# Three of a row's eight routed weight pairs through seven half-row block products, and layer 1 with its channels on the partitions

## The reference, cut to what matters

```python
def _gemma_mlp(x, gate_w, up_w, down_w):
    g = jnp.einsum('bsh,hi->bsi', x, gate_w)
    u = jnp.einsum('bsh,hi->bsi', x, up_w)
    return jnp.einsum('bsi,ih->bsh', jax.nn.gelu(g, approximate=True) * u, down_w)
...
rw = jax.nn.softmax(router_logits, axis=-1)
w, sel = jax.lax.top_k(rw, 2)
w = w / w.sum(axis=-1, keepdims=True)
...
x = x + sum_e dense_w[:, e] * mlp_e(x) + mlp_shared(x)
out = jnp.einsum('btc,oc->bto', x, W_base) + b_base
h = jnp.einsum('btc,erc->bter', x, As)
lora = jnp.einsum('bter,eor,be->bto', h, Bs, w)
x = x + out + lora * 2.0
```

## Time and profile before

| | |
|---|---|
| median of three runs | 812.03 us (811.63 to 812.24) |
| the profiled execution | 812.84 us |
| its span, first to last instruction | 811.0 us |
| TensorE busy | 804.5 us (99%), granted clock 1.00 in every slice |
| VectorE busy | 557.0 us (69%) |
| ScalarE busy | 402.1 us (50%) |
| GpSimd busy | 85.9 us (11%) |
| DMA | 80.34 MB, mean 99 GB/s |

### The profile page before, as it was taken

How to read it: one execution, slowest core, us unless ns; L and a number is a source line. 1 busy time by engine, 2 the same in 40 slices (tenths; PEclk the granted TensorE clock), 3 DMA queues, 4 the chain that set the end, 5 groups by cost and what they waited for, 6 DMA issues and landing times.

```text
span 811.0 us, 11123 instructions
## 1 busy us (share of the span) xinstructions
PE 804.5 (99%) x3666; PEld 670.8 (83%) x3666; DVE 557.0 (69%) x808; ACT 402.1 (50%) x659; POOL 85.9 (11%) x66
## 2 busy tenths in 40 slices
PE   9999999999999999999999999999999999999998
PEld 7788888888887888888888888888888888888886
DVE  4886987987876575666766666665666656667554
ACT  5574564554653544445445445444454445454442
POOL 1441321321111000100100010010001001001000
PEclk9999999999999999999999999999999999999999
DMA  6330521303211723433343244244225333333200
GB/s 200 86 113 12 147 77 18 114 0 104 91 39 53 221 87 108 131 118 103 104 146 102 78 147 125 79 132 138 93 88 167 91 104 129 121 99 104 66 0 27
DMA packets 92293, 80.34 MB, mean 99 GB/s; under 512 B 32864, under 2 KB 85856, under 8 KB 92256
## 3 DMA queue, kind: packets, MB, share of 16 engines
q1 hardware_dynamic: 92256, 79.88, 31.9%
HBM read 67.28 MB, written 12.58 MB: 98 GB/s over the span
## 4 chain that ended last, share of the span: by engine, by line
PE 98%; DVE 1%; ACT 0%; issue 0%; POOL 0%; DVEq 0%; ACTq 0%; POOLq 0%
PE ps_ring L587 61%; PE ps_acc L587 34%; PE ps_ring L707 1%; PE ps_acc L767 0%; DVE wide L1122 0%; PE ps_acc L701 0%; DVE xc L1122 0%; DVE sh_dn L1122 0%; ACT wide L872 0%; PE ps_acc L787 0%; PE ps_ring L605 0%; DVE stage L1456 0%; ACT stage L967 0%; PE ps_ring L609 0%; PE ps_ring L613 0%
## 5 line engine op out<-in xcount | busy, mean ns | idle before, releaser
L587 PE MATMUL ps_ring<-xc,wide 128*128 128x512 f32 x2220 | 529.4, 389 | 0.3 <-DVE post L1164 0.3
L587 PEld LDWEIGHTS ps_ring<-xc,wide 128*128 128x128 f32 x2220 | 415.6, 188 | 86.3 <-issue 0.7
L872 ACT CAST inner_hi<-post 128x512 fp32r<-128x512 f32 x192 | 118.1, 622 | 295.6 <-DVE post L1385 229.5
L1122 DVE TENSOR_TENSOR inner_lo<-post,inner_hi 128x512 fp32r<-128x512 f32 x192 | 135.5, 713 | 88.5 <-ACT inner_hi L872 88.2
L587 PE MATMUL ps_acc<-inner_hi,wide 128*128 128x512 f32 x504 | 175.8, 389 | 0.9 <-ACT stage L967 0.9
L1385 DVE SCALAR_TENSOR_TENSOR post<-post,coef_now,ps_ring 128x512 f32<-128x512 f32 x128 | 95.3, 744 | 55.8 <-PE ps_ring L587 54.8
L587 PEld LDWEIGHTS ps_acc<-inner_hi,wide 128*128 128x128 f32 x504 | 94.6, 188 | 21.0 <-ACT stage L967 1.4
L587 PE MATMUL ps_acc<-inner_lo,wide 128*128 128x512 f32 x252 | 98.0, 389 | 0.0
L1071 ACT ACTIVATE post<-ps_ring 128x512 f32<-128x512 f32 x128 | 76.0, 594 | 39.9 <-PE ps_ring L587 39.8
L1122 DVE TENSOR_TENSOR wide<-xbuf,wide 128x1024 fp32r<-128x1024 f32 x64 | 68.8, 1115 | 24.8 <-ACT wide L872 24.8
L1122 DVE TENSOR_TENSOR wide<-raw,wide 128x1024 fp32r<-128x1024 f32 (+2 forms) x70 | 64.4, 957 | 30.9 <-ACT wide L872 30.9
(11 more groups left out here) (100 smaller groups left out, 415.2 us busy)
## 6 DMA issues: line engine op xcount, KB each, us to landing
raw<-n_L_cond_skill_gate_dram SPq DMA_DIRECT2D x32, 256.0 KB, 2.9
raw<-in_L_cond_skill_up_dram SPq DMA_DIRECT2D x32, 256.0 KB, 3.5
raw<-n_L_cond_skill_down_dram SPq DMA_DIRECT2D x32, 256.0 KB, 3.8
xbuf<-n_L_cond_skill_gate_dram SPq DMA_DIRECT2D x32, 256.0 KB, 2.9
xbuf<-in_L_cond_skill_up_dram SPq DMA_DIRECT2D x32, 256.0 KB, 3.4
xbuf<-n_L_cond_skill_down_dram SPq DMA_DIRECT2D x32, 256.0 KB, 3.7
xt_scratch<-xbuf SPq DMA_DIRECT2D x8, 512.0 KB, 3.3
sh_scratch<-stage SPq DMA_DIRECT2D x8, 512.0 KB, 2.7
```

The lines of the kernel that those rows point to most:

```text
L587: last = pe.matmul(dst, left_[a], right_[b], start=start and n == 0, stop=stop and n == len(PASSES) - 1, skip_group_check=adds)
L872: return nc.scalar.copy(dst, src)
L1122: return V.tensor_tensor(dst, src, hi.bitcast(F32), ALU.subtract)
```

## The change

Pairs 3, 5 and 7 of each row (`SEVEN`) no longer make 4 times 6 matmuls of 512 columns for gate and up. Instead the row's tokens are cut in two halves of 256 (`HS`), each weight in its four 128 by 128 blocks, and `seven_products` makes seven products, each of them for gate and for up side by side in one bank: 7 x 2 x 3 = 42 matmuls of 256 columns. Both chunks of the pair are done at once; then come the two `down` that are due. For this

- POOL makes the sums of the tokens once a row (`sums_of_x`, 4 operations of 256 columns) and of the weights for each of the three pairs (`sums_of_weights`, 4 operations of 256 columns), and one of the output blocks (`ex_c22`, 512 columns); ACT and DVE split the sums (1024 columns each time);
- ACT copies two banks out (`ex_copy_out`), DVE adds four times a bank (`ex_seven`), and gelu and multiply work on pieces of 256, 256 and 512 columns;
- the weights of a pair are split in one piece of 1536 columns, at the chunks of a table (`SPLIT_AT`), and the splits stand ahead of the chunk's own `inner_lo` instead of behind it; for pairs 3, 5 and 7 `weights_ready` comes with the split of the sums;
- `layer1` of rows 0 to 6 makes 12 matmuls of 512 columns with the channels on the partitions; ACT adds the bias (`add_bias`), DVE transposes within blocks of 32 (`turn_output`), and SP stores a row in 8 transfers of 64 KB with runs of 128 bytes (`store_blocks`);
- `fold` goes from chunk 12 to chunk 9, `w_eff` from chunks 13 and 14 to 12 and 13, and layer 1's constants are loaded earlier in row 0 and to other memory; they are still taken in at one chunk of row 0 (`CONST_STEP`), now chunk 4 instead of 7.

```diff
+    SEVEN = [3, 5, 7]
+    NS = len(SEVEN)
+    HS = S // 2
...
+        SPLIT_AT = {0: 2, 2: 3, 5: 4, 6: 5, 9: 6, 10: 7, 13: 8, 14: 9}
+        SUMS_AT = {2 * pr - 2: n_s for n_s, pr in enumerate(SEVEN)}
...
+            def sums_of_weights(b, n_s):
+                s_, j = divmod(SEVEN[n_s], PAIRS)
+                st = b * NS + n_s
+                pool.wait_ge(raw_landed[j], b * (48 * TOP_K) + 48 * (s_ + 1))
+                pool.wait_ge(weights_ready, b * (TOP_K * PAIRS) + (SEVEN[n_s - 1] + 1 if n_s else SEVEN[-1] + 1 - TOP_K * PAIRS))
+                v = raw_gu(j).rearrange("p (g c i) -> p g c i", g=2, c=HC)
+                a11, a12 = v[:, :, 0, P:PW], v[:, :, 1, P:PW]
+                a21, a22 = v[:, :, 0, 0:P], v[:, :, 1, 0:P]
+                s1, s2, s3, s4 = (s_tmp[:, :, n, :] for n in (S1, S2, S3, S4))
+                G.tensor_tensor(s1, a21, a22, ALU.add).then_inc(ex_s1_made, 1)
+                G.tensor_tensor(s3, a11, a21, ALU.subtract)
+                pool.wait_ge(ex_s1_made, 2 * st + 1)
+                G.tensor_tensor(s2, s1, a11, ALU.subtract).then_inc(ex_s1_made, 1)
+                pool.wait_ge(ex_s1_made, 2 * st + 2)
+                G.tensor_tensor(s4, a12, s2, ALU.subtract).then_inc(ex_s_made, 1)
...
+            def ex_c22(b, n_s):
+                st = b * NS + n_s
+                pool.wait_ge(ex_v_done, st + 1)
+                pool.wait_ge(ex_u1_done, st + 1)
+                G.tensor_tensor(ex_v, ex_v, ex_u1, ALU.add).then_inc(ex_c22_done, 1)
...
+            def row(b, first):
+                sums_of_x(b, first)
+                sums_of_weights(b, 0)
                 pool.wait_ge(base_landed, b * 16 + 16)
-                pool.wait_ge(xf_landed, b * 16 + 16)
                 G.tensor_tensor(base, base, xf, ALU.add).then_inc(base_ready, 1)
-            with pool.Fori(0, B) as i:
-                row(i)
+                for n_s in range(NS):
+                    ex_c22(b, n_s)
+                    if n_s < NS - 1:
+                        sums_of_weights(b, n_s + 1)
+            row(0, True)
+            with pool.Fori(1, B) as i:
+                row(i, False)
...
+            def seven_products(b, par, k, n_s):
+                st = b * NS + n_s
+                for n, (bank, a_, b_, opens) in enumerate(PRODUCTS):
+                    if n == 0:
+                        pe.wait_ge(gelu_done, whole(b, k - 1))
+                    elif n == 1:
+                        pe.wait_ge(ex_t_ready, b + 1)
+                        pe.wait_ge(mul_done, whole(b, k - 1))
+                    elif n == 2:
+                        pe.wait_ge(mul_done, whole(b, k))
+                    elif n == 3:
+                        pe.wait_ge(gelu_done, whole(b, k))
+                    elif n in (4, 5):
+                        pe.wait_ge(ex_copied, 2 * st + n - 3)
+                    else:
+                        pe.wait_ge(ex_v_done, st + 1)
+                    for part in (GATE, UP):
+                        last = product(ring[bank][:, part * HS:(part + 1) * HS],
+                                       [ex_left(n_s, hl, part, a_) for hl in range(2)],
+                                       [ex_right(par, hl, b_) for hl in range(2)],
+                                       opens and part == GATE, True, True)
+                    last.then_inc(ex_product, 1)
+            def down_chunk(k):
...
             def layer1(b):
                 pe.wait_ge(x1_ready, b + 1)
                 pe.wait_ge(w_eff_ready, b + 1)
-                for t in range(TT):
+                for m in range(HC):
                     for c in range(HC):
-                        last = product(ps_misc[t // 2][:, t % 2 * H:(t % 2 + 1) * H],
-                                       [v[:, c, t * P:(t + 1) * P] for v in x1_s],
-                                       [w[:, c * H:(c + 1) * H] for w in w_eff_s], c == 0, c == HC - 1)
-                    if t % 2 == 1:
-                        last.then_inc(l1_done, 1)
+                        last = product(ps_misc[m][:], [w[:, c * H + m * P:c * H + (m + 1) * P] for w in w_eff_s],
+                                       [v[:, c, :] for v in x1_s], c == 0, c == HC - 1)
+                    last.then_inc(l1_done, 1)
...
+                    if k // 2 in SEVEN:
+                        if k % 2 == 0:
+                            seven_products(b, par, k, SEVEN.index(k // 2))
+                            down(b, k - 2)
+                            down(b, k - 1)
+                        continue
...
             def split_routed(b, s, j, freed, count):
-                split_routed_gu(b, s, j, freed, count)
-                split_routed_dn(j)
+                act.wait_ge(raw_landed[j], b * (48 * TOP_K) + 48 * (s + 1))
+                act.wait_ge(freed, count)
+                take_hi(ex_all(0, j), raw[j]).then_inc(weights_hi, 1)
...
+            def ex_copy_out(b, n_s, first):
+                st = b * NS + n_s
+                if n_s == 0:
+                    if first:
+                        act.wait_ge(turned_w, 1)
+                        act.wait_ge(a_ready, 1)
+                    else:
+                        act.wait_ge(o_ready, b * 2)
+                for n, to, bank in ((0, ex_u1, 0), (1, ex_v, 2)):
+                    act.wait_ge(ex_product, st * NP + n + 1)
+                    if n == 0:
+                        act.wait_ge(ex_mul, 3 * st)
+                    nc.scalar.copy(to, ring[bank][:]).then_inc(ex_copied, 1)
...
+            def ex_gelu_of(b, k, n_s):
+                st = b * NS + n_s
+                act.wait_ge(ex_product, st * NP + 5)
+                act.wait_ge(mul_done, whole(b, k))
+                gelu_of(gelu[0][:, 0:HS], ring[0][:, 0:HS]).then_inc(ex_gelu, 1)
+                act.wait_ge(ex_c_done, 2 * st + 1)
+                gelu_of(gelu[0][:, HS:S], ex_c12[:, 0:HS]).then_inc(ex_gelu, 1)
+                act.wait_ge(ex_c_done, 2 * st + 2)
+                act.wait_ge(ex_c22_done, st + 1)
+                gelu_of(gelu[1].rearrange("p (t n) -> p t n", t=2), ex_c2[:, :, 0:HS]).then_inc(ex_gelu, 1)
...
+            def ex_seven(b, k, n_s):
+                st = b * NS + n_s
+                s = k // IC
+                dve.wait_ge(ex_product, st * NP + 3)
+                dve.wait_ge(ex_copied, 2 * st + 2)
+                V.tensor_tensor(ex_v, ring[3][:], ex_v, ALU.add).then_inc(ex_v_done, 1)
+                dve.wait_ge(ex_product, st * NP + 4)
+                V.tensor_tensor(ex_u1, ring[1][:], ex_u1, ALU.add).then_inc(ex_u1_done, 1)
+                dve.wait_ge(ex_gelu, 3 * st + 1)
+                dve.wait_ge(inner_ready, b * K + k)
+                ex_inner(b, s, inner[0][:, 0:HS], gelu[0][:, 0:HS], ring[0][:, HS:S])
+                dve.wait_ge(ex_product, st * NP + 6)
+                dve.wait_ge(ex_u1_done, st + 1)
+                V.tensor_tensor(ex_c12, ring[2][:], ex_u1, ALU.add).then_inc(ex_c_done, 1)
+                dve.wait_ge(ex_product, st * NP + 7)
+                dve.wait_ge(ex_c22_done, st + 1)
+                V.tensor_tensor(ex_u1, ring[3][:], ex_u1, ALU.add).then_inc(ex_c_done, 1)
+                dve.wait_ge(ex_gelu, 3 * st + 2)
+                dve.wait_ge(ex_c_done, 2 * st + 1)
+                ex_inner(b, s, inner[0][:, HS:S], gelu[0][:, HS:S], ex_c12[:, HS:S])
+                dve.wait_ge(ex_gelu, 3 * st + 3)
+                dve.wait_ge(ex_c_done, 2 * st + 2)
+                ex_inner(b, s, inner[1].rearrange("p (t n) -> p t n", t=2),
+                         gelu[1].rearrange("p (t n) -> p t n", t=2), ex_c2[:, :, HS:S])
                 for i in range(2):
-                    dve.wait_ge(l1_done, b * 2 + i + 1)
-                    V.tensor_tensor(o_row[:, 2 * i:2 * i + 2, :],
-                                    ps_misc[i][:].rearrange("p (t h) -> p t h", t=2),
-                                    bias[:].unsqueeze(1).to_broadcast([P, 2, H]), ALU.add)\
-                        .then_inc(o_ready, 1)
+                    dve.wait_ge(inner_hi, b * K + k + i + 1)
+                    take_lo(inner_s[1][:, k % 4 + i, :], inner[i], inner_s[0][:, k % 4 + i, :])                        .then_inc(inner_ready, 1)
             def row(b, par, first, last):
+                def split_pair(k):
...
-                take_lo(ex_gu_all(1, j), raw_gu(j), ex_gu_all(0, j))
-                take_lo(ex_dn_all(1, j), raw_dn(j), ex_dn_all(0, j)).then_inc(weights_ready, 1)
+                last = take_lo(ex_all(1, j), raw[j], ex_all(0, j))
+                if s * PAIRS + j not in SEVEN:
+                    last.then_inc(weights_ready, 1)
```

More of the change, by code:

```diff
@@ L480, in row @@
                         .then_inc(layer1_landed, 16)
+                    store_shared(Q - 1)
+                else:
+                    sp.wait_ge(x1_done, b * 2)
+                    sp.wait_ge(sh_stored, 16 * B)
+                    sp.dma_start(base, sh_dram[b]).then_inc(base_landed, 16)
+                load_routed(b, 1, range(2, PAIRS))
                 if not last:
@@ L830, in row @@
```

(20 more changed lines are left out.)

264 lines of the change are left out of this document (193 added, 71 removed).

## The result

The changed kernel takes **806.35 us** (median of 6 runs, 805.82 to 807.56) beside 812.13 for the kernel before (6 runs, 811.56 to 812.41). The ratio is 0.9932, 95% interval 0.9922 to 0.9942: 0.7% faster. The forecast was 807.8 (801.2 to 815.0), with a chance of 0.66 for faster. The profiled execution has a span of 804.7 us where the one before had 811.0.

What follows compares the result with a forecast made beforehand. TensorE, busy throughout the routed stage, was taken as the bound. Terms -9.5 - 1.1 + 4.9 + 1.5 = -4.2 took the profiled 812.84 to 808.6, stated as 807.8 us against the 812.03 median; range 801.2 to 815.0.

Steps and rivals of the forecast that it cites:

- seven products, 24 pairs: TensorE's gate and up: a pair falls from 5.44 to 5.04 us, 24 times over 8 rows: -9.5 us.
- `layer1`, 7 rows: TensorE in rows 0 to 6: 2.88 us becomes 2.72, 0.16 x 7 = -1.1 us.
- wait for `layer1_sum`: TensorE idle 0.7 us before the next row's first down, seven times: +4.9 us.
- row 0: Layer 1's constants and both first splits of sums in chunk 4 delay pair 3's product 2: +1.5 us.
- the walk: Pair 7's first product to the next row's first down: TensorE wants x1_done at 18.64 us, VectorE finishes at 19.3.
- turns: VectorE operations with both inputs in SBUF wait for GpSimd's whole operation: 0.55 us each, six before layer1_sum.
- All of it arrives: Rival: two turns fewer, or VectorE 0.7 us earlier at the walk's start; full -10.6 gives 801.4 us; chance 0.18.
- Given back: Rival: one turn more, TensorE waiting 1.07 to 1.5 us a row; 810.4 to 813.7 us; chance 0.17.
- Slower: VectorE becomes the bound: Rival: multiplies reading a bank also take turns with GpSimd, up to 1.0 us more per row: 814.8 us; chance 0.17.
- It doesn't do what it says: Rival: 256-column matmuls take over 129 ns between waits; chance counted within the given-back and slower cases.

Runs made afterwards that it cites:

- experiment 4: Kernel before with the change's layer 1 alone (512-column matmuls, bias on ScalarE, transposes, eight stores): 811.0 us, ratio 0.9984.
- experiment 1: The change with GpSimd's four sums of the next row's tokens made to wait until behind layer1_sum: 802.14 us, ratio 0.9874.
- Experiment 5: Kernel before with, in row 0 alone, pair 2's split ahead of chunk 0's high and low parts: 810.76 us, ratio 0.9988.
- experiments 2 and 10: 2: the change with GpSimd's token and weight sums on 8 columns, 800.56 us; 10: the change with token sums behind layer1_sum and CONST_STEP = 3, 800.89 us.
- experiment 9: The change with one of GpSimd's four token sums made on 8 of 256 columns in rows 1 to 7: 803.21 us, ratio 0.9891.
- experiment 8: The change with one more 256-column sum on GpSimd ahead of the token sums in rows 1 to 7: 810.2 us, ratio 0.9976.
- experiment 7: The change with the copy of three columns (coef_now) moved from VectorE to ScalarE, ahead of chunk 0's gelu: 806.78 us, ratio 0.9934.

## Why the prediction was right, and where it was off

| term | forecast | measured |
|---|---|---|
| seven products, 24 pairs | -9.5 | 24 x (68.74 - 67.58) / 3 = -9.3, by the rows of experiments 4 and 1 |
| `layer1`, 7 rows | -1.1 | 7 x 0.18 = -1.3 by rows, -1.2 by medians (experiment 4) |
| wait for `layer1_sum` | 7 x 0.7 = +4.9 | 7 x 0.62 = +4.3 |
| row 0 | +1.5 | +1.5 (1.28, and four small ones of 0.45 in all where the kernel before has two of 0.2) |
| split of pair 2 ahead, row 0 | none | -1.1 |
| sum | -4.2 | -5.9; measured -5.8 by medians, -6.3 by spans |

Of the 6.3 us between the spans 0.7 lie ahead of 44 us, where both kernels do the same; behind it the difference is 5.6. The forecast's 9.5 should read 9.6, 24 times its 0.40. The matmuls of seven products take 5.03 us, which would make 9.8; a row shows a little less saved, 0.39 us a pair. The splits in one piece and the earlier `fold` had no experiment of their own, and the sum leaves next to nothing for them.

**The place and the mechanism were right.** TensorE's matmuls were spaced as forecast, 0.120, with waits every six; the formula in the Trainium skill (TensorE: Matmul & The Clock Gate, Back-to-back issue gap) that the forecast set beside this, 0.109 and a saving of 14.4, is given there for a single isolated matmul, and the page says that a stream of weight loads and matmuls is spaced otherwise. So the forecast was wrong to put it down as that page's estimate for this stream, and right to go by its rows. In each row TensorE waits at the one place of the walk. The walk set TensorE's wish for `x1_done` at 18.64 us behind the first product of pair 7; in row 0 that product begins at 310.08, and 328.74 - 310.08 = 18.66. It put the end of `layer1_sum` at 19.3; it is 329.15 - 310.08 = 19.07. VectorE came to the first addition at 3.5 instead of 3.7, and the number of turns was six as counted. That it came to six holds some luck: one of them is on the copy of three columns, which the walk did not treat as an operation that can be held. The wait was forecast 0.1 us a row too large, which is 0.6 us of the error.

**What the forecast lacked** is a term for a wait that goes away. It walked row 0 for waits that the change adds and did not ask which waits of row 0 it takes away, though the kernel before has one there of 1.1 us, the largest of its routed stage. Experiment 5 shows that it is the place of pair 2's split. It is most of the 1.45 us between 807.8 and 806.35. The cause of row 0's added wait was named only in half: the constants and both splits stand there, but without the long turn with `base` (2.4 us), which the forecast did not place there, they would not have mattered.

**The rivals.** *All of it arrives* is the state that experiments 2 and 10 reach, with 800.6 and 800.9 against its 801.4, and experiment 1 but for row 0's wait, with 802.1. It had asked for two turns fewer; one fewer took the wait down to 0.1 (experiment 9), since the wait was smaller than forecast. *Given back* is one turn more: experiment 8 has it and measures 810.2, 0.2 below that rival's 810.4 to 813.7. *Slower: VectorE becomes the bound* is refuted in its mechanism: 80 multiplies that read up from a bank and the coefficient from SBUF last 733 to 750 ns, also at 392.51, where one of GpSimd's sums runs beside it. By the Trainium skill (SBUF — State Buffer, Who interferes with whom) a VectorE instruction with at most one input in SBUF does not contend, outside the modes that take both ports; the trace says that here a column of scalars did not count as a second one. *It doesn't do what it says* did not happen.

Whether fewer turns could be had by another order of VectorE's own operations around `layer1_sum` was not tried.

## What to carry to other kernels

An engine that is busy 90% of the time is late at particular places, and the count that decided here is how many of its operations were held by another engine's just there: moving four sums of a mostly idle engine by some microseconds was worth two fifths of the matmul time that the change saved. Before adding work to an idle engine, walk the stretch in front of the next wait of the bounding engine, and see whether that work can stand behind it. And when an order is changed, list the waits of the old order too: one that disappears counts as much as one that is added. Where a difference of 1 us matters, compare profiles from a point at which both kernels have done the same, not by their spans alone.

## What the runs showed that was not expected

- A copy of three columns, one input in SBUF, is held like an operation with two: 699 to 705 ns in the seven rows where GpSimd's sums run beside it, 170 in row 0, where none does, and 161 to 171 ns in all rows when the sums are moved (experiment 1). The same section of the Trainium skill says that copies can run in a mode that takes both ports and then contend. The trace agrees in that this copy is held; no trace here shows its mode. The forecast had priced it at 0.17.
- A multiply that reads a bank gives GpSimd a free slot: its last sum took 0.74 us there and 2.24 beside a split. Removing a short operation ahead of such a slot moved the turn and saved 0.2 instead of 0.5 us (experiment 7).
- GpSimd's operation can lose more than VectorE's: L688 took 2.25 us behind a split of 1.75, while VectorE lost 0.54.
- ScalarE stands 2.2 to 2.3 us for issue (waiting for nothing that the profile shows) when the loop of two rows turns. It is hidden in the change, and one more instruction there lengthened it by 1.2 us and brought it onto TensorE's path.
